# Grouped attention: both squaring passes of a raw head on ScalarE, GpSimd left with the subtraction

## The reference, cut to what matters

```python
ln_out = _ln(hidden_states, ln_w, ln_b)
q  = _ln(_fp8_linear_pertensor(ln_out, wq,  wq_scale,  q_in_scale ).reshape(b, s, g, hpg, d), qln_w,  qln_b)
k  = _ln(_fp8_linear_pertensor(ln_out, wk,  wk_scale,  k_in_scale ).reshape(b, s, g, d),      kln_w,  kln_b)
v  = _fp8_linear_pertensor(ln_out, wv, wv_scale, v_in_scale).reshape(b, s, g, d)
core = _gqa(q, k, v).reshape(b, s, nh * d)
qx = _ln(_fp8_linear_pertensor(ln_out, wqx, wqx_scale, qx_in_scale).reshape(b, s, g, hpg, d), qxln_w, qxln_b)
kx = _ln(kx.reshape(b, sc, g, d), kxln_w, kxln_b)      # kx, vx from the context
xout = _gqa(qx, kx, vx).reshape(b, s, nh * d)
```

## Time and profile before

| | us |
|---|---|
| median of 3 runs | 2110.52 (2108.07 to 2111.7) |
| the profiled execution | 2108.4 |
| its span | 2106.6 |
| TensorE busy (matmul) | 2022.6 (96%) |
| VectorE busy | 1481.3 (70%) |
| ScalarE busy | 1183.6 (56%) |
| GpSimd busy | 660.9 (31%) |

### The profile page before, as it was taken

One profiled execution on the slowest core, in us unless ns is written; L12 is line 12 of the kernel. 1 busy time (PEld: TensorE's weight loads), 2 busy tenths in 40 slices (PEclk: granted clock), 3 DMA queues, 4 the chain that ended last, 5 costly groups with the idle time before them and its releaser, 6 DMA issues. The chain is left out here.

```text
span 2106.6 us, 31981 instructions
## 1 busy us (share of the span) xinstructions
PE 2022.6 (96%) x11352; PEld 1576.0 (75%) x11352; DVE 1481.3 (70%) x3345; ACT 1183.6 (56%) x3027; POOL 660.9 (31%) x635
## 2 busy tenths in 40 slices
PE   8999899999999999999998999999999999998998
PEld 5645778888888888888876886665666785666997
DVE  2397778878787878787666837676677667885555
ACT  2073677777777777777764444553544446773332
POOL 1300344444444344444430002323341101222442
PEclk9999999999999999999999999999999999999999
DMA  4033433332424242332332203323322220002300
GB/s 182 22 118 109 142 108 114 95 120 86 144 73 142 84 135 79 116 102 81 105 99 80 96 1 146 117 85 125 115 105 112 85 71 22 2 2 101 125 1 32
DMA packets 60176, 193.71 MB, mean 92 GB/s; under 512 B 9409, under 2 KB 28641, under 8 KB 56049
## 3 DMA queue, kind: packets, MB, share of 16 engines
q1 hardware_dynamic: 48498, 172.16, 24.4%
q10 hardware_dynamic: 9504, 8.50, 1.4%
q0 software_dynamic: 2016, 11.01, 1.3%
HBM read 171.75 MB, written 19.49 MB: 91 GB/s over the span
## 5 line engine op out<-in xcount | busy, mean ns | idle before, releaser
L977 PE MATMUL psum<-la_w_both,context 128*128 128x256 f32 (+1 forms) x1536 | 343.6, 380 | 0.0
L977 PEld LDWEIGHTS psum<-la_w_both,context 128*128 128x128 f32 (+1 forms) x1536 | 277.3, 184 | 44.9
L1440 POOL TENSOR_TENSOR norm_std<-room 128x400 f32<-128x400 f32 x74 | 66.8, 902 | 251.7 <-DVE room L1203 251.7
L936 PE MATMUL psum<-qa_xqf,qa_two 128*128 128x400 f32 x640 | 142.2, 365 | 2.9 <-DVE qa_mv L1379 2.9
L936 PEld LDWEIGHTS psum<-qa_xqf,qa_two 128*128 128x128 f32 x640 | 119.2, 190 | 8.1 <-DVE qa_mv L1379 3.8
L3011 ACT ACTIVATE it_prob<-psum,it_nm 100x257 f32<-100x257 f32 (+1 forms) x256 | 101.7, 412 | 40.3 <-DVE it_nm L3042 40.2
L1127 ACT ACTIVATE qa_prob<-psum,qa_nm 100x361 f32<-100x361 f32 x128 | 71.8, 561 | 77.5 <-DVE qa_nm L1303 77.5
L1464 POOL TENSOR_TENSOR qa_yt<-qa_yb,qa_ym 128x400 f32<-128x400 bf16 x64 | 60.2, 941 | 164.8 <-DVE qa_ym L1336 164.8
L995 PE MATMUL psum<-qa_kxT,room 128*100 128x361 f32 x256 | 100.4, 474 | 10.9 <-DVE la_w_kt L1326 9.6
L1433 POOL TENSOR_TENSOR room<-room,qa_inv 128x500 f32<-128x500 f32 x64 | 83.3, 1302 | 62.0 <-DMA qa_inv<-qa_std_rows 53.6
L1300 DVE TENSOR_REDUCE qa_mx<-psum 100x2 f32<-100x722 f32 x64 | 58.2, 910 | 54.2 <-PE psum L996 54.1
(11 more groups left out here) (399 smaller groups left out, 5297.0 us busy)
## 6 DMA issues: line engine op xcount, KB each, us to landing
context<-in_context SPq DMA_DIRECT2D x70, 722.0 KB, 5.1
qa_inv<-qa_std_rows SPq DMA_DIRECT2D x64, 250.0 KB, 3.9
qa_w_raw<-in_qa_w SPq DMA_DIRECT2D x8, 1536.0 KB, 16.6
la_gf_raw<-in_gf_w SPq DMA_DIRECT2D x16, 768.0 KB, 4.7
qa_piece<-in_tf_pieces ACTq DMA_DIRECT2D x64, 128.0 KB, 2.0
la_w_qt<-in_qa_o SPq DMA_DIRECT2D x8, 1024.0 KB, 5.0
gf_ternary<-la_gf_made POOLq DMA_DIRECT2D x7, 768.0 KB
gf_ternary<-keep POOLq DMA_DIRECT2D x7, 768.0 KB
```

The costliest lines, as they stand in the source:

```text
L936: mm = pe.matmul(psum[:, bank, 0:HALF], two[:, part, j, k, :], xqf[:, PART_XQ[j], k, (h % 2) * HALF:(h % 2 + 1) * HALF], start=(k == 0 and ...
L977: mm = pe.matmul(psum[0:rows, i // 2, (i % 2) * 256:(i % 2) * 256 + 256], ctxT[:, n % 2, k, t0:t0 + rows], kv_raw[:, s, k, :], start=(k == ...
```

## The change

ScalarE now squares each raw head once into `square` in fp32, waits for that, and a second activation (Copy) rounds it into the high part of `split`. The multiplication is gone from VectorE (6 units) and from GpSimd (74 units), and with it their waits for `raw_ready` and for the square. ScalarE has a new wait for the previous unit's subtraction (`lo_ready`), as there is one `square` buffer, and waits for `last_rows_saved` before its first unit.

```diff
@@ ScalarE, high_squares(u)
                 act.wait_ge(S_["raw_ready"], u + 1)
                 if u >= 2:
                     act.wait_ge(S_["var_mm"], u - 1)
-                act.activation(split[:, u % 2, 0, :], raw_of(u), ACT.Square).then_inc(S_["hi_ready"], 1)
+                if u:
+                    act.wait_ge(S_["lo_ready"], u)
+                act.activation(square, raw_of(u), ACT.Square).then_inc(S_["sq_ready"], 1)
+                act.wait_ge(S_["sq_ready"], u + 1)
+                act.activation(split[:, u % 2, 0, :], square, ACT.Copy).then_inc(S_["hi_ready"], 1)
@@ ScalarE, before the first units
             for r in range(2):
                 load_piece(r, r)
+            act.wait_ge(last_rows_saved, 16)
             for u in FIRST:
                 high_squares(u)
@@ VectorE, first_low_squares(u)
-                dve.wait_ge(S_["raw_ready"], u + 1)
-                if u:
-                    dve.wait_ge(S_["lo_ready"], u)
-                dve.tensor_tensor(square, raw_of(u), raw_of(u), ALU.mult).then_inc(S_["sq_ready"], 1)
-                dve.wait_ge(S_["sq_ready"], u + 1)
                 dve.wait_ge(S_["hi_ready"], u + 1)
                 dve.tensor_tensor(split[:, u % 2, 1, :], square, split[:, u % 2, 0, :], ALU.subtract).then_inc(
                     S_["lo_ready"], 1)
@@ GpSimd, low_squares(u)
-                pool.wait_ge(S_["raw_ready"], u + 1)
-                pool.wait_ge(S_["lo_ready"], u)
-                pool.tensor_tensor(square, raw_of(u), raw_of(u), ALU.mult).then_inc(S_["sq_ready"], 1)
-                pool.wait_ge(S_["sq_ready"], u + 1)
                 pool.wait_ge(S_["hi_ready"], u + 1)
                 pool.tensor_tensor(split[:, u % 2, 1, :], square, split[:, u % 2, 0, :], ALU.subtract).then_inc(
                     S_["lo_ready"], 1)
```

## The result

| | before | after |
|---|---|---|
| median, us | 2109.73 (20 runs) | 2114.53 (20 runs) |
| ratio to before, 95% interval | | 1.0023 (1.0014 to 1.0031) |
| span of the profiled execution, us | 2106.6 | 2109.9 |

The changed kernel is 4.8 us slower (0.23%; the interval allows 3.0 to 6.5), where 4.5 us was forecast. Measured once more beside others it gave 1.0021 (1.0010 to 1.0033). The three runs that the forecast started from had their median 0.8 us above that of the twenty.

A forecast was written before the change was run, and what follows sets the result against it. TensorE's list was taken to bound the kernel (111.58 of 114.20 us busy per group). Terms 3.0 + 0.2 + 1.1 + 0.2 = 4.5 us on the median 2110.52 gave 2115.0, range 2108 to 2121.

The forecast's parts named there:

- Part 1: GpSimd's multiplication goes in 74 units: L1295 0.83 to 0.22 us, VectorE's `pT` 0.61 earlier, nothing gained past `pT`.
- Part 2: Second ScalarE activation in the steps: `pT` 0.57 us later in step 21; 1.1 us from `b` = 1 steps, 0.2 from `kxT`.
- serial: Rival: ScalarE's pair or its hand-offs cost more than 0.57 us; 2119 at +0.1, 2123 at +0.2; chance 0.22.
- Part 3: Six first units: squaring and rounding now in series, +0.50 us each, last subtraction 3.0 us later, nothing taking it up.
- head hidden: Rival: transfers step 0 waits for anyway take up the 3.2 us before and in step 0; 2111.8; chance 0.11.
- Step 0: In step 0 `nrm_x` can start at 220.29 instead of 220.10, behind Square and Copy: +0.2 us.
- Ports: Rival: freed VectorE lets L1014 start 0.24 us earlier in 40 steps, 9.6 us, giving 2105.4; chance 0.10.
- Clock: Rival listed with chance 0.07, nearly all counted as slower; the prediction given states no mechanism or size for it.

The follow-up runs named there:

- first_new: The kernel before with the new two-activation form on the six first units only; 2113.05 us, ratio 1.0019 (1.0010 to 1.0028).

## Why the prediction was right

- **Part 1, GpSimd.** L1295 went to 0.22 us in the steps and VectorE's `pT` came earlier, with nothing gained past `pT`: L1342 idles 0.71 us until `project_out` ends. As forecast.
- **Part 2, ScalarE in the steps.** Square, wait and Copy added 0.57 us, and L1014 was forecast 0.02 earlier; it came 0.06 earlier. The term that was off is the hand-off from ScalarE's `pT` to TensorE: 0.05 us, not the 0.10 that the earlier trace rows show for `kxT`. In the `b` = 1 steps L1014 comes 1.75 us behind the raw copy (before 1.65), +0.10 and not +0.16. A full group is 0.10 to 0.13 longer, and from step 2 to step 62 that makes 0.8 us, where 6 x 0.16 + 0.2 = 1.2 was forecast for the same steps. Further down the list `nrm_x` moved by 0.45 in step 21, as forecast. The rival "serial" needed the same term larger; it was smaller.
- **Part 3, the first units.** Forecast 3.0 us: 0.50 for each of six. The copies are 2.23 apart, 0.49 more. `project_context` of step 0 came 2.9 and 3.3 us later in the two traces, and no transfer took it up, so "head hidden" is out.
- **Step 0.** With it and step 1 the traces show 3.0 to 3.8 at L1014 of step 1, depending on the two that are compared, where 3.0 + 0.2 + 0.16 was forecast. `first_new` had 4.8 there, so this mark moves with more than the six units.
- **"Ports".** Rightly rejected for this change, for the reason given: ScalarE's half of `pT` takes VectorE's place. But its price was put at 9.6 us, and the freed VectorE is worth 12.6 us by the traces (the medians say 16, with 13 to 20 allowed). The step that failed is the 0.24 us a step times 40: it left out steps 1 to 5, where TensorE stands 1.55 us with no `project_out` ahead and gained 0.6, and the `b` = 1 steps, where it stands 0.47 and L1014 gained as much.
- **"Clock".** One part of it showed: in the changed kernel the lower level also covers part of 214 to 218 (0.75 in the first trace), where the kernel before had none, and instead the fall behind step 0 came later or not at all. My reading that a stall of 2.08 us does not lower the clock was wrong; the kernel before, once more, had its fall at that very stall.

The sum of the traces is 4.1 us against 4.5 forecast: the steps cost less than forecast and the start as much. The medians say 4.8 and allow 3.0 to 6.5; how the last 0.7 us divides can't be settled at this scatter, so that 4.8 lies so near 4.5 is in part luck.

## What to carry to other kernels

Work moved off a nearly idle engine gains only what it had held up elsewhere, and if it goes into the list of an engine that feeds the bound, it eats the margin there. Here the multiplication had held up VectorE, which was worth 12 us or more, and the longer list of ScalarE took all of it back. A second activation more then cost another 20 us. Look instead for a small operation that takes several times its usual time beside a large one of the neighbour; here one more wait, which moved the large one by 0.4 us, was worth 12 us with no work moved at all. Such an operation costs time only where TensorE ends up waiting for it. There is another in this kernel: L1303, on 4 elements, takes 0.17 to 0.19 us in 17 steps, and 1.22 or 1.23 in 17 others, where GpSimd's L1433 starts just ahead of it. The exponentials wait for it. In the steps with a unit TensorE never waits for what comes of them. In four of the last steps, which have no unit, L1303 takes 0.88 or 0.89 us and TensorE waits for the probabilities behind it at L1004, 0.20 us twice and 1.5 us twice. By these rows up to 1.8 us could be had there (an estimate, 0.2 + 0.2 + 0.7 + 0.7); no run here tried it. And look at the start-up form of a loop apart from its steady form: there the two engines had worked side by side, and six units in series cost more than seventy-four in the steps.

## What the hardware showed that was not expected

- Whether TensorE's clock falls at a given stall varies from one execution to the next of the same kernel: at 2.08 us of idle ahead of L1014 of step 1 it stayed at 1.00 in one trace of before and went to 0.73 in the other.
- TensorE starts 0.05 us behind ScalarE's `pT` and 0.10 behind ScalarE's `kxT`, both copies out of PSUM. The difference was not looked into.
- Contention between VectorE and GpSimd cost time only where TensorE waited for VectorE. With the multiplication behind `pT`, L1268 grew from 0.53 to 0.95 us and the time stayed.

The Trainium skill (SBUF — State Buffer, "Who interferes with whom") says that the contention is an exclusive lock, taken by whichever operation starts first. The traces agree. L1295 has 0.83 us when the multiplication starts 0.04 ahead of it, and 0.22 us when it starts 0.35 behind, when L1295 is over. Both orders also show in the kernel before, with VectorE first in the first pair and GpSimd first in the second:
```profile
243.07 0.68 DVE L1253 TENSOR_TENSOR qa_two<-qa_w_raw,qa_two 128x512 fp32r<-128x512 f32 x1
243.09 1.37 POOL L1440 TENSOR_TENSOR norm_std<-room 128x400 f32<-128x400 f32 x1
...
369.84 1.24 POOL L1433 TENSOR_TENSOR room<-room,qa_inv 128x500 f32<-128x500 f32 x1
369.88 1.23 DVE L1303 TENSOR_SCALAR qa_nm<-qa_mx 100x4 f32<-100x4 f32 x1
```
L1253 keeps its 0.68 us, and the multiplication grows from 0.85 to 1.37, in each of the 7 places where they meet so. The one that comes second ends a little behind the first (L1295 0.02 us behind the multiplication, and not its own 0.22), so not all of it was held.
